# Cross-attention and quantised feed-forward, one core: 361 keys cut into chunks of 122, 120 and 119 plus a zero key, in place of 121, 120 and 120

## The reference

```python
q = rmsnorm((layernorm(x) @ Wq).reshape(B, Sq, H, D), gq)
k = rmsnorm((ctx @ Wk).reshape(B, Skv, H, D), gk)
v = (ctx @ Wv).reshape(B, Skv, H, D)
attn = softmax(einsum("bqhd,bkhd->bhqk", q, k) / sqrt(D))
x = x + einsum("bhqk,bkhd->bqhd", attn, v).reshape(B, Sq, H * D) @ Wo
# act_quant: 8 bits per token; weight_quant: ternary; fwht: Hadamard rotation
x = x + h_bitlinear(silu(h_bitlinear(ln(x), w_gate)) * h_bitlinear(ln(x), w_up), w_down)
```

## Time and profile before

| | us |
|---|---|
| median of 3 runs | 1418.27 (1416.5 to 1418.69) |
| span of the profiled execution, first to last instruction | 1415.7 |
| PE busy in it | 1384.3 (98%) |
| PE weight loads (overlapping) | 1192.2 (84%) |
| DVE busy | 933.8 (66%) |
| ACT busy | 940.2 (66%) |
| POOL busy | 517.2 (37%) |

### The profile page before, as it was taken

One profiled execution on the slowest core, in us unless ns is written; L12 is line 12 of the kernel. 1 busy time (PEld: TensorE's weight loads), 2 busy tenths in 40 slices (PEclk: granted clock), 3 DMA queues, 4 the chain that ended last, 5 costly groups with the idle time before them and its releaser, 6 DMA issues. The chain is left out here.

```text
span 1415.7 us, 25806 instructions
## 1 busy us (share of the span) xinstructions
PE 1384.3 (98%) x8407; PEld 1192.2 (84%) x8407; DVE 933.8 (66%) x2399; ACT 940.2 (66%) x2072; POOL 517.2 (37%) x323
## 2 busy tenths in 40 slices
PE   8999988999999999999999999999989999999998
PEld 8889867999999999999999999998867677776775
DVE  5222036667777777777777777766457677776775
ACT  4566558888888888888888888887533433343332
POOL 0033324432233223332323332324645465655551
PEclk9999999999999999999999999999989999999999
DMA  6867823334443443444344344325443322233211
GB/s 219 215 189 220 226 54 91 100 111 117 128 112 114 134 128 114 116 124 134 107 124 117 113 133 128 106 82 172 126 153 79 86 60 67 61 97 75 60 30 42
DMA packets 173492, 165.05 MB, mean 117 GB/s; under 512 B 81440, under 2 KB 149040, under 8 KB 171568
## 3 DMA queue, kind: packets, MB, share of 16 engines
q1 hardware_dynamic: 166448, 150.82, 38.5%
q10 hardware_dynamic: 6912, 12.59, 2.7%
HBM read 123.44 MB, written 33.01 MB: 111 GB/s over the span
## 5 line engine op out<-in xcount | busy, mean ns | idle before, releaser
L764 POOL TENSOR_TENSOR rk_sp<-ms_sp,neg_half 76x10 f32<-76x10 f32 (+1 forms) x128 | 238.5, 1880 | 567.0 <-DMA ms_sp<-ms 567.0
L1194 DVE CUSTOM_DVE_ANT_0 sc<-psS,rk 100x361 f32<-100x361 f32 x256 | 136.4, 533 | 97.1 <-PE psS L839 71.3
L986 ACT ACTIVATE pr<-ex,ri 100x361 f32<-100x361 f32 x256 | 153.6, 600 | 63.6 <-DVE ri L1184 63.6
L979 ACT ACTIVATE ex<-sc,nb,rq_all 100x361 f32<-100x361 f32 x256 | 175.9, 687 | 7.8 <-DVE nb L1203 7.8
L867 PE MATMUL psZ<-pT_hi,cK_hi 120*128 120x400 f32 (+1 forms) x384 | 133.3, 347 | 0.0
L867 PE MATMUL psZ<-pT_hi,cK_lo 120*128 120x400 f32 (+1 forms) x384 | 132.4, 345 | 0.0
L867 PE MATMUL psZ<-pT_lo,cK_hi 120*128 120x400 f32 (+1 forms) x384 | 132.2, 344 | 0.0
L852 PEld LDWEIGHTS psP<-ident,pr 100*120 100x120 f32 (+1 forms) x768 | 80.2, 165 | 43.5 <-issue 35.3
L839 PE MATMUL psS<-ring_hi,q_hi 128*100 128x362 f32 x256 | 97.0, 379 | 5.0 <-DVE mx L1194 5.0
L852 PE MATMUL psP<-ident,pr 100*120 100x100 f32 (+1 forms) x768 | 96.5, 261 | 4.0 <-ACT pr L986 4.0
L1176 DVE TENSOR_TENSOR pT_lo<-psP,pT_hi 121x600 fp32r<-121x600 f32 x128 | 99.0, 773 | 1.5 <-ACT pT_hi L1010 1.5
(11 more groups left out here) (295 smaller groups left out, 3947.6 us busy)
## 6 DMA issues: line engine op xcount, KB each, us to landing
rk<-rk_dram SPq DMA_DIRECT2D x64, 564.1 KB
q_dram<-q_out SPq DMA_DIRECT2D x64, 200.0 KB, 4.3
q_in<-q_dram SPq DMA_DIRECT2D x64, 200.0 KB, 5.2
o_dram<-o SPq DMA_DIRECT2D x64, 200.0 KB, 5.4
stage<-in_w_ff SPq DMA_DIRECT2D x12, 1024.0 KB, 6.3
w_in<-in_w_ff ACTq DMA_DIRECT2D x48, 256.0 KB, 2.4
o_in<-o_dram SPq DMA_DIRECT2D x12, 1024.0 KB, 5.9
cT_in<-in_ctxT SPq DMA_DIRECT2D x15, 361.0 KB, 5.4
```

Source lines behind the costliest of these rows:

```text
L764: nc.gpsimd.tensor_tensor(rk_sp[:, cols], ms_sp[:, cols], neg_half[0:HG * SKR, :].to_broadcast([HG * SKR, n]), op=ALU.pow).then_inc(g_rk, 1)
L979: nc.scalar.activation(ex[:, h % 2, :], sc[:, h % 2, :], ACT.Exp, bias=nb[:, h % 2:h % 2 + 1], scale=factor(n), accum_out=rs[:, h % 2:h % ...
L986: nc.scalar.activation(pr[:, h, :], ex[:, h % 2, :], ACT.Copy, scale=ri[:, h % 2:h % 2 + 1]).then_inc(a_pr, 1)
L1194: nc.vector.tensor_tensor_reduce(out=sc[:, h % 2, :], in0=psS[0:SQ, 0:SK], in1=rk[:, u % 2, h, :], scale=1.0, scalar=-3.0e38, op0=ALU.mult ...
```

## The change

The chunks become 122, 120 and 120 wide (`KW`), starting at keys 0, 122 and 242 (`KO`). These are 362 columns for 361 keys, so the last chunk has 119 real keys and one zero key. `KR`, the number of real keys, takes the place of `KW` in the DMAs that load the context. `pr` becomes 362 columns wide for each head, and its last column is set to zero once by DVE; the last context row of the third chunk is set to zero once by POOL, which clears 32 partitions of the third chunk before SP loads the first context. The order and the number of all other instructions on every engine stay as they were.

```diff
-KW = [121, 120, 120]
-KO = [0, 121, 241]
+KW = [122, 120, 120]
+KR = [122, 120, 119]
+KO = [0, 122, 242]
...
             sp.dma_start(cT_next[:], ctxT[1].rearrange("(c p) k -> p c k", p=P)).then_inc(d_c, 16)
+            sp.wait_ge(g_const, 5)
             for i in range(3):
-                sp.dma_start(weights["cK_in"][0:KW[i], i, :], ctx_k[0, KO[i]:KO[i] + KW[i], :]).then_inc(d_cK, 16)
+                sp.dma_start(weights["cK_in"][0:KR[i], i, :], ctx_k[0, KO[i]:KO[i] + KR[i], :]).then_inc(d_cK, 16)
...
             nc.gpsimd.memset(weights["ones"][:], 1.0).then_inc(g_const, 1)
+            pool.wait_ge(g_const, 4)
+            nc.gpsimd.memset(weights["cK_in"][3 * QW32:P, 2, :], 0.0).then_inc(g_const, 1)
+            pool.wait_ge(g_const, 5)
...
-        ex, pr = sb("ex", [SQ, 2, SK]), sb("pr", [SQ, HG, SK])
+        ex, pr = sb("ex", [SQ, 2, SK]), sb("pr", [SQ, HG, SKP])
...
-                src = [ctx_k[bass.ds(b, 1), KO[i]:KO[i] + KW[i], :].rearrange("a k c -> k (a c)") for i in range(3)]
+                src = [ctx_k[bass.ds(b, 1), KO[i]:KO[i] + KR[i], :].rearrange("a k c -> k (a c)") for i in range(3)]
                 sp.wait_ge(v_cK, b)
                 for i in range(3):
-                    sp.dma_start(cK_in[0:KW[i], i, :], src[i]).then_inc(d_cK, 16)
+                    sp.dma_start(cK_in[0:KR[i], i, :], src[i]).then_inc(d_cK, 16)
...
                 if isinstance(pair, int) and pair == 0:
-                    pe.wait_ge(v_zero, 1)
+                    pe.wait_ge(v_zero, 2)
...
-                nc.scalar.activation(pr[:, h, :], ex[:, h % 2, :], ACT.Copy, scale=ri[:, h % 2:h % 2 + 1]
+                nc.scalar.activation(pr[:, h, 0:SK], ex[:, h % 2, :], ACT.Copy, scale=ri[:, h % 2:h % 2 + 1]
...
         @block.vector
         def _(dve):
+            nc.vector.memset(pr[:, :, SK:SKP], 0.0).then_inc(v_zero, 1)
             nc.vector.memset(psP[:], 0.0).then_inc(v_zero, 1)
```

## The result

The changed kernel takes 1463.46 us (1460.41 to 1469.05, 5 runs), the kernel before in the same session 1416.5 us (1414.4 to 1418.69, 5 runs). The ratio is 1.033, 95% interval 1.0308 to 1.0351. The forecast was 1413.3 us. The change lost 47 us where it was to gain 5.

A forecast was written before the change was run, and what follows sets the result against it. The prediction took PE to bound the attention stage. Savings of 5.7 us at PE less 0.7 given back made 5.0, additions counted 0, so 1418.27 - 5.0 = 1413.3 us, range 1411.6 to 1418.6.

The forecast's parts named there:

- What bounds the kernel: Attention stage: PE, busy for all 640.00 us, sets the pace; what it saves should come out nearly whole.
- Second 121: Fourth of six transpose loads in each half: 19 ns exposed beside a short transpose, 128 halves, 2.4 us saved.
- First 121 of a second half: First transpose load of a second half, uncovered on a drained PE: 42 ns saved, times 64, 2.7 us.
- The small terms and the give-back: Attention-stage transposes: covered loads save 0.2 us, loads waiting for ACT 0.4 us; late and just-in-time units lose 0.7 us.
- the covered load: First transpose load of a first half, covered by a key matmul: 3 ns times 54, 0.2 us saved.
- the first halves that wait for ACT: First transpose load of first halves where PE waits for `pr`: 10 in the stage, 42 ns each, 0.4 us saved.
- rival 2: Attention stage: ACT takes over, PE's saving is waited off in half the units, 2.0 us lost; 1414.6 us; chance 0.10.
- The sign that I had named for rival 2: PE's waits for `pr` in the attention stage at more than 4 us, instead of staying near 1.3 us.
- The rate: PE's transpose loads: 122 columns load at the fast rate, 133 to 138 ns, not 183; 121 misses it.
- Rival 1: PE's transpose loads: 122 columns, no multiple of 4, load slowly; nothing saved, 0.2 us cost, 1418.5 us; chance 0.20.
- What the change adds: Memsets on DVE and POOL, SP's wait, DMAs of the same 361 rows, one more partition: 0, at most 0.2 us.
- rival 3: PE's 120-column transposes: odd pitch or start made them fast, four more slow gaps per half; 9.7 us, 1428; chance 0.03.

The follow-up runs named there:

- the two runs with equal cuts: Context loaded as 128, 128 and 112 + 8 rows under the old widths, 1415.46 us; as 128, 128 and 112 + 7 under the changed widths, 1411.22 us.
- the cuts spread: The changed kernel with its context rows loaded as 128, 128 and 112 + 7 rows: 1411.22 us, ratio 0.997.

## Why the prediction was wrong, step by step

- **What bounds the kernel**: right. PE sets the pace of the attention stage, and with good loads what it saved came out at the end: 4.2 us between the two runs with equal cuts (1415.46 and 1411.22; they ran on different chips, where the kernel before took 1415.18 and 1415.08).
- **Second 121**: 19 ns forecast; the largest matmul of an undisturbed first half went from 268 to 250, so 18 to 20. Right.
- **First 121 of a second half**: 42 ns forecast from the transposes of line 303; 347 to 304 is 43. Right.
- **The small terms and the give-back**: 0.2 us for the covered load and 0.4 us for the first halves that wait for ACT, less 0.7 us given back. Together with the two terms above they made 5.0 us; measured are 4.2 us, about 2.6 either way (the two intervals together), so neither the small terms nor rival 2, whose saving was 3.7 us, can be judged by the time. The sign that I had named for rival 2 did not come: with the cuts spread, the waits of PE's loads for `pr` between 260 and 900 us are 1.9 us, against 1.3 before.
- **The rate**: the even loads are fast and the odd ones slow, which holds for 106, 120, 122 and 128 against 119 and 121. Rival 1 (multiples of four) was wrong. The one rate for all loads that the Trainium skill gives, page "TensorE: Matmul & The Clock Gate", section "LDWEIGHTS (loading the stationary operand)", does not hold for these transposes: 122 columns take 138 ns and 121 take 182.
- **What the change adds**: this is the step that failed. The prediction says "The DMAs move the same 361 rows" and counts them at 0. The bytes are the same, but the number of engines fell, by the packet counts, from 41 to 24 over the three loads, and that cost some 50 us: one row more in one DMA costs 32 us by itself, and with the rows cut otherwise the loss is gone. I weighed the added memsets and waits, which cost nothing that shows, and passed over the one edit that looked like renaming, `KR` for `KW` in the DMAs. Of a DMA whose shape changes, the shape is to be costed, not only the bytes.
- **No slack named**: the second half of the same step. I never asked which loads land just in time. It was there to be read: seven loads with landings of up to 6.2 us against a use 6.3 to 6.9 us after the issue.
- **The rivals**: the one on the slow side, rival 3, had a mechanism that the runs exclude (the 120s at new starts and pitch take 141 ns in the mean, where they took 156). None of the four named a transfer, and the place where the prediction would have looked for a loss, behind 983 us, is not where it lies: 44.1 of the 46.0 us are in the attention stage. That rival 3 decides "from about one and a half more slow loads per half on" doesn't follow from its numbers either: at 2.4 us for each (19 ns x 128) it takes two to undo a gain of 5.0 us.

Sizes: the waits of ACT, 34.1 us for `cT_in` and 7.2 more than before for `cK_in`, became 31.8 us of added idle time on PE and some 16.5 us of slow clock, against 4.2 us of gain.

What stays open: why 127 rows on one engine don't take twice as long as 122 on two (the packet records show 6.3 to 7.3 us from the first to the last of the rows with 127, 4.4 to 7.7 us in the changed kernel and 2.3 to 4.3 us in the kernel before), and how much of the delay of `cT_in` is its own transfer and how much its later start. With 127 rows part of it is the issue: SP gets the third load of context rows out 1.5 to 4.5 us behind the second, where all three take 1.27 us in the rows of the kernel before, above. The number of engines itself is inferred, from the packet counts of all twelve kernels, with nine different sums of engines, which fit to the packet; no view names the engines.

## What to carry to other kernels

When an edit changes the row count of a DMA, factor the number: by the packet counts 128, 112 and 120 rows spread over 16, 16 and 15 engines, while 122 and 127 sit on two and on one, and what follows in the queue pays. Choose tile sizes for the compute engine and for the DMA together (128, 128, 106 serves both), or load other rows than the tile has. And look for loads with no slack before you touch what stands in front of them in the queue: here waits of 2.7 to 6.2 us in seven places made most of a loss of 47 us, as an in-order engine passes them on and the clock falls behind most of the stalls.

## What the runs showed of the hardware that I had not expected

- The weight load of an fp32 transpose was fast at the four even widths tried and slow at the two odd ones: 131 ns for 106 columns, 138 for 120 and 122, 141 for 128, but 184 for both 119 and 121. The fast loads grow by 10 ns over 22 columns, 0.45 ns a column. The 46 ns between 138 and 184 are close to one more such step for each of the 120 columns, so the odd widths look like half the rate; that is an estimate.
- One row more in one DMA (121 to 122) cost 32 us of 1415, six more (127) 79 us. With seven more (128), and the other two chunks loaded as 128 and 112 + 8 rows, it cost nothing.
- Behind each of the six stalls of PE of 2.6 to 4.4 us in the attention stage PE ran at 1.2 GHz for a while: the mean granted clock of the attention stage fell from 1.00 to 0.98, about 17 us of the loss. The stall of 2.23 us left it at 1.00.
